# Sixteen experts' sums gathered, normed and stored in four groups of four instead of two batches

## The chip, the core and the metric

The kernel runs on one core of a Trainium2 chip. A core has TensorE (matrix products), VectorE, ScalarE and GpSimd (called POOL in the profile), each with an instruction queue of its own, worked in order, and SyncE, which here only starts transfers. Sixteen DMA engines move data between HBM and the on-chip memory. The engines meet at semaphores: an instruction or a landed transfer raises one, and another queue waits until it has a value. The metric is the device time of one execution in microseconds; smaller is better.

## The reference

Input x has 2 batches of 4096 tokens with 256 numbers each. Two layers follow each other, each as x = x + layernorm(layer(layernorm(x))). The first is a state-space layer (Mamba); the change doesn't touch it. The second is a mixture of 16 experts:

```
router_logits = silu(h @ router_w1) @ router_w2
expert_probs = softmax(router_logits.transpose(0, 2, 1), axis=-1)       # over the tokens
expert_weights, token_indices = top_k(expert_probs, 64 per batch and expert)
gate  = silu(expert_inputs @ w1);  value = expert_inputs @ w2
weighted = ((gate * value) @ w3) * expert_weights
output = zeros.at[token_indices].add(weighted)
x = x + layernorm(output)
```

A token may be chosen by several experts; their outputs are summed before the norm, so a token's norm needs its last expert. Every input and output is float32.

## The kernel before

`scan_layers` (nearly 2000 us) makes the state-space layer, the router and the part of the output that no expert touches. `experts` (L1256 to L1589) follows, and only it is changed. It handles 128 rows (64 tokens of two batches) per expert and runs these queues side by side.

VectorE ranks the logits (L1341 to L1378) and hands POOL the places of the chosen tokens in a table.

POOL starts every indirect transfer, one row per partition: `find` (L1526) fetches an expert's 128 row numbers from the table, `take` (L1529) its tokens' hidden rows and x rows, `add` (L1535) adds an expert's weighted outputs onto the rows of a sum buffer in HBM (`combine_scratch`), `gather` (L1539) reads summed rows back, `store` (L1549) writes final rows to the output. Each `take(e)` waits for its own find and is followed by `find(e + 3)`. An add waits for its expert's product (`s_y`) and for all adds before it (`d_add`), since two adds onto one row must not cross.

TensorE (L1477) makes for each expert the transposes of its tokens, `pg` (gate) and `pv` (value), and the product of the expert before. Two buffers of each let the next expert's `pg` and `pv` run while VectorE multiplies gate by value (L1421) and ScalarE makes silu (L1468) and the weighting (L1455). SyncE loads the last five experts' weights when an earlier expert's product has left its room (L1328).

Each row of the sum buffer has extra columns in which the adds leave a power of two per expert. `statistics` (L1387) reads from them whether a later expert has the same token: then this expert is a loser for the row, and its store is sent out of bounds (`dest`). So a group may be gathered when its own experts are added, and the row is stored by the last expert that holds it among those added. A later store of the same row must come after the earlier one (the wait on `d_fin`, L1554).

The sums come back in groups `GROUPS = ((0, 5), (5, 10), (10, 13), (13, 16))`. Before add 10, POOL gathers experts 0 to 9 and waits until they have landed, because add 10 changes the same rows. VectorE has `statistics(0)` behind multiply 14 and everything else behind multiply 15 (L1422 to L1434); `inverse` (L1543) is POOL's power -1/2 of the variances; `mean` (L1407) is a small VectorE step; the scaling itself is on ScalarE (`normalised`, L1457), behind the last weighting; `total` (L1413) adds x. Stores 0 to 9 stand behind adds 12 to 15 (two, two, three, three). After add 15, experts 10 to 15 are gathered, normed and stored.

## Time and profile before

| | us |
|---|---|
| median of three runs | 2185.17 |
| lowest, highest run | 2182.62, 2185.49 |
| span of the profiled execution | 2180.9 |
| busy in the span: VectorE, POOL, TensorE, ScalarE | 1878.9, 1810.3, 1681.2, 1411.6 |
| HBM read, written | 77.82 MB, 39.52 MB |

The profiled execution is one of its own; its page gives its span, from the first to the last instruction, and no further time. A run's time holds the span and what lies around it: 4.27 us between the span and the median here.

The page gives one line per group of instructions: line of the program, engine, operation, output and inputs, count, busy time, mean duration, and the idle time before. The timeline gives the instructions of one engine in order of time; what stands in brackets is the idle time before an instruction and what ended it. "issue" there means that the engine waited for nothing that the profile shows. The chain of waits goes back from the last instruction to what released it. A transfer's landing is counted from the start of the instruction that issues it.

### The profile page before, as it was taken

How to read it: one execution, taken by the hardware profiler on the slowest of the kernel's cores; microseconds unless marked ns; L12 is line 12 of the kernel's file. 1: busy time of each engine (PE TensorE's matmuls, PEld its weight loads, DVE VectorE, ACT ScalarE, POOL GpSimd, SP SyncE). 2: the span in 40 equal slices, each digit the busy share in tenths (PEclk: the TensorE clock that was granted, in tenths of full speed). 3: DMA queues.
4: the chain of work that ended last, by engine and by line, in shares of the span. 5: the costliest groups of instructions: out<-in, count | busy, mean ns of one | idle time of the engine just before them, and what ended most of it. 6: DMA issues, size and time to landing. Idle time of an engine off the chain costs nothing. (4 is left out here: it accounts for less than half of the span.)

```text
span 2180.9 us, 23218 instructions
## 1 busy us (share of the span) xinstructions
PE 1681.2 (77%) x5620; PEld 648.2 (30%) x5620; DVE 1878.9 (86%) x2070; ACT 1411.6 (65%) x2547; POOL 1810.3 (83%) x770
## 2 busy tenths in 40 slices
PE   7777879887888978788879787978888884651690
PEld 3222323232232323232323232323232231220690
DVE  2477999999999999999999999999999999996221
ACT  2565676867686768777777777776867685531121
POOL 0275999999998989898989999999999998950556
PEclk9897979889898979798979798989889895665795
DMA  2663367676667585757475656667576667427742
GB/s 92 163 181 86 88 136 158 129 159 137 146 146 154 126 175 113 167 114 166 108 159 136 146 137 144 154 136 157 126 151 148 137 139 152 110 73 234 245 106 63
DMA packets 168981, 305.16 MB, mean 140 GB/s; under 512 B 27648, under 2 KB 87810, under 8 KB 168864
## 3 DMA queue, kind: packets, MB, share of 16 engines
q1 hardware_dynamic: 137696, 240.13, 44.6%
q0 software_dynamic: 30784, 62.85, 16.1%
q10 hardware_dynamic: 384, 1.05, 0.2%
q14 instruction: 96, 0.79, 0.1%
q8 instruction: 21, 0.34, 0.1%
HBM read 77.82 MB, written 39.52 MB: 54 GB/s over the span
## 5 line engine op out<-in xcount | busy, mean ns | idle before, releaser
L1022 DVE TENSOR_TENSOR_SCAN room<-pa,carry,room 128x512 f32<-128x512 f32 x1024 | 1243.4, 1263 | 69.8 <-ACT pa L871 56.1
L1221 POOL TENSOR_TENSOR room<-room 128x2048 f32<-128x2048 f32 x256 | 1172.7, 4591 | 144.2 <-ACT carry L864 144.2
L871 ACT ACTIVATE pa<-room,neg_a 128x512 f32<-128x512 f32 x1024 | 695.1, 687 | 352.7 <-DVE room L1022 338.6
L520 PE MATMUL py<-room,blk 128*32 128x512 f32 x2048 | 338.8, 734 | 150.5 <-DVE gate L1028 95.8
L1008 DVE TENSOR_TENSOR room<-room,pb 128x2048 f32<-128x2048 f32 x192 | 434.0, 2260 | 0.8 <-DMA room<-du 0.8
L1214 POOL TENSOR_TENSOR room<-room,b_rep 128x2048 f32<-128x2048 f32 x64 | 290.3, 4536 | 6.5 <-DVE room L1022 4.6
L584 PE MATMUL pp<-xs,w_dtx 128*128 128x512 f32 x512 | 254.0, 631 | 18.0 <-DVE du L951 11.7
L593 PE MATMUL pb<-bc,sel_b 32*128 32x512 f32 x288 | 204.3, 796 | 66.2 <-DVE room L1008 66.2
L548 PE MATMUL pp<-xsp,w_conv 128*128 128x512 f32 x512 | 242.2, 606 | 8.4 <-ACT xsp L738 8.4
L540 PE MATMUL pp<-xnt,w_in 128*128 128x512 f32 x256 | 170.2, 800 | 71.7 <-ACT xs L745 59.4
L520 PEld LDWEIGHTS py<-room,blk 128*32 128x32 f32 x2048 | 44.7, 117 | 347.8 <-issue 222.5
L584 PEld LDWEIGHTS pp<-xs,w_dtx 128*128 128x128 f32 x512 | 96.4, 199 | 170.0 <-issue 142.9
L1187 POOL TENSOR_TENSOR du<-du,xs 128x512 f32<-128x512 f32 x64 | 79.7, 1263 | 74.0 <-DVE du L960 74.0
L548 PEld LDWEIGHTS pp<-xsp,w_conv 128*128 128x128 f32 x512 | 92.8, 191 | 150.1 <-issue 102.0
L564 PE MATMUL po<-xnt,w_in 128*128 128x512 f32 x240 | 125.3, 647 | 7.6 <-ACT gate L750 7.6
L607 PE MATMUL po<-w_out,gate 128*128 128x256 f32 x512 | 124.0, 391 | 4.1 <-DVE z L983 3.3
L593 PEld LDWEIGHTS pb<-bc,sel_b 32*128 32x128 f32 x288 | 51.6, 222 | 210.1 <-issue 122.8
L607 PEld LDWEIGHTS po<-w_out,gate 128*128 128x128 f32 x512 | 96.1, 193 | 51.1 <-issue 33.5
L540 PEld LDWEIGHTS pp<-xnt,w_in 128*128 128x128 f32 x256 | 55.0, 238 | 172.0 <-ACT xs L745 97.2
L745 ACT ACTIVATE xs<-pp,cb 128x512 f32<-128x512 f32 x64 | 43.6, 681 | 73.8 <-PE pp L548 69.2
L1421 DVE TENSOR_TENSOR act<-act,pv 128x512 f32<-128x512 f32 x16 | 11.0, 688 | 80.8 <-PE pv L1512 80.8
L769 ACT ACTIVATE du<-pp 128x512 f32<-128x512 f32 x64 | 38.0, 594 | 57.2 <-PE pp L584 49.5
(185 smaller groups left out, 1860.0 us busy)
## 6 DMA issues: line engine op xcount, KB each, us to landing
room<-du SPq DMA_DIRECT2D x1016, 128.0 KB, 2.4
du<-du POOLq DMA_DIRECT2D x56, 512.0 KB, 6.5
room<-in_L_ffn_w_dram SPq DMA_DIRECT2D x39, 512.0 KB, 7.4
room<-bc_scratch SPq DMA_DIRECT2D x64, 256.0 KB, 5.0
du<-late POOLq DMA_DIRECT2D x28, 512.0 KB, 6.3
combine_scratch<-zeros SPq DMA_DIRECT2D x16, 520.0 KB, 9.7
xt<-in_L_attn_x_dram SPq DMA_DIRECT2D x16, 512.0 KB, 4.4
b_rep<-bc_scratch SPq DMA_DIRECT2D x64, 128.0 KB, 5.4
```

The lines of the kernel that those rows point to most:

```text
L520: mm = pe.matmul(py[32 * j:32 * j + 32, :], blk[:], h[:, quad % 4, j, :], start=(g == 0), stop=(g == 3), tile_position=(0, 32 * j))
L540: mm = pe.matmul(pp[:], w_in[:, k, m * P:(m + 1) * P], xnt[:, k, :], start=(k == 0), stop=(k == KC - 1))
L548: mm = pe.matmul(pp[:], w_conv[:, m, tap, :], xsp[:, m % 2, tap:tap + T], start=(tap == 0), stop=(tap == TAPS - 1))
L564: mm = pe.matmul(residual_bank(i, m), w_in[:, k, DI + m * P:DI + (m + 1) * P], xnt[:, k, :], start=(k == 0), stop=(k == KC - 1))
L584: mm = pe.matmul(pp[:], w_dtx[:, k, c * P:(c + 1) * P], xs[:, k, :], start=(k == 0), stop=(k == DC - 1))
L593: pe.matmul(pb[:, bank, :], sel_b[b:b + 32, g, :], bc[b:b + 32, :], start=True, stop=True, tile_position=(b, 0)).then_inc(s_brep, 1)
L607: mm = pe.matmul(po[:, (s % 2) * DM:(s % 2 + 1) * DM], gate[:, par, k, s * P:(s + 1) * P], w_out[:, k, :], start=(k == 0), stop=(k == DC - 1))
L871: act.activation(pa[:, decay_bank(t), :], rep[:, c % 2, t % 4, 0, :], ACT.Exp, scale=neg_a[:, a_column(t):a_column(t) + 1]).then_inc(s_exp, 1)
L1008: v.tensor_tensor(bq[:, quad % 2], rep[:, c % 2, :, 1, :], pb[:, pb_bank, :].unsqueeze(1).broadcast_to((P, 4, T)), ALU.mult).then_inc(s_bd, 1)
L1022: v.tensor_tensor_scan(h[:, quad % 4, t % 4, :], pa[:, decay_bank(t), :], bq[:, quad % 2, t % 4, :], carry[:, par, t:t + 1], ALU.mult, ALU ...
L1214: pool.tensor_tensor(bq[:, 1], rep[:, c % 2, :, 1, :], b_rep[:, g // 2, :].unsqueeze(1).broadcast_to((P, 4, T)), ALU.mult).then_inc(s_bp, 1)
L1221: pool.tensor_tensor(h[:, quad % 4], h[:, quad % 4], c_rep[:, par, quad % 4, :].unsqueeze(1).broadcast_to((P, 4, T)), ALU.mult).then_inc(s ...
```

## The change

`GROUPS` becomes four groups of four. POOL gathers group g before add 4, 8 and 12 (and after add 15), waits for the landing ahead of that add, makes the group's power two experts later (or at the end), and stores its rows two behind each of two adds. The statistics of a group stand on VectorE behind the multiply two experts after the group, its mean, its norm (now on VectorE, four `tensor_scalar`) and its sums behind the multiply after that, but none later than behind multiply 15. ScalarE's `normalised` goes. The row numbers are copied to float per group. Of the finds ahead of the first take, two remain instead of three; a take is followed by `find(e + 2)`.

```
-    GROUPS = ((0, 5), (5, 10), (10, 13), (13, 16))
-    HALF = 10
+    GROUPS = ((0, 4), (4, 8), (8, 12), (12, 16))
+    STATS_AFTER, TOTAL_AFTER = 2, 3
+    STORES_AFTER = {6: (0, 1), 7: (2, 3), 10: (4, 5), 11: (6, 7), 14: (8, 9), 15: (10, 11)}
...
                 def statistics(g):
                     first, stop = GROUPS[g]
-                    if g == 0:
-                        v.tensor_copy(rowf[:], rowid[:]).then_inc(s_lose, 1)
                     v.wait_ge(d_cb[g], 16 * (stop - first))
+                    v.tensor_copy(rowf[:, first:stop], rowid[:, first:stop])
...
+                    v.wait_ge(s_lose, g + 1)
+                    v.scalar_tensor_tensor(out=dest[:, first:stop], in0=loser[:, first:stop], scalar=float(2 * B * S),
+                                           in1=rowf[:, first:stop], op0=ALU.mult, op1=ALU.add).then_inc(s_dest, 1)
                     v.wait_ge(s_f, 2 * g + 2)
                     v.tensor_scalar(fvar[:, first:stop], fmv[:, first:stop, 1], EPS, None, ALU.add).then_inc(s_fv, 1)
...
+                def total(g):
                     first, stop = GROUPS[g]
                     v.wait_ge(s_fp, g + 1)
                     v.scalar_tensor_tensor(out=fnm[:, first:stop], in0=fmv[:, first:stop, 0], scalar=-1.0,
                                            in1=frs[:, first:stop], op0=ALU.mult, op1=ALU.mult).then_inc(s_fn, 1)
-                def total(g):
-                    for e in range(*GROUPS[g]):
+                    v.wait_ge(s_fn, g + 1)
+                    for e in range(first, stop):
+                        v.tensor_scalar(comb[:, e, 0:DM], comb[:, e, 0:DM], frs[:, e:e + 1], fnm[:, e:e + 1], ALU.mult,
+                                        ALU.add).then_inc(s_fa, 1)
+                    for e in range(first, stop):
                         v.wait_ge(s_fa, e + 1)
                         v.tensor_tensor(comb[:, e, 0:DM], comb[:, e, 0:DM], taken[:, e, DM:], ALU.add).then_inc(s_fo, 1)
...
                     v.tensor_tensor(act1[:, e % 2, :], act1[:, e % 2, :], pv[:, e % 2, :], ALU.mult).then_inc(s_m, 1)
-                    if e == 14:
-                        statistics(0)
-                statistics(1)
...
-                total(3)
+                    for g, (_, stop) in enumerate(GROUPS[:-1]):
+                        if e == min(stop + STATS_AFTER, E - 1):
+                            statistics(g)
+                        if e == min(stop + TOTAL_AFTER, E - 1):
+                            total(g)
+                statistics(len(GROUPS) - 1)
+                total(len(GROUPS) - 1)
...
-                for g in range(len(GROUPS)):
-                    normalised(g)
...
-                    if e + 3 < E:
-                        find(e + 3)
+                    if e + 2 < E:
+                        find(e + 2)
...
-                for e in range(3):
+                for e in range(2):
                     find(e)
...
                 for e in range(E):
+                    before = [g for g, (_, stop) in enumerate(GROUPS) if stop == e]
+                    for g in before:
+                        pool.wait_ge(d_add, 16 * e)
+                        for done in range(*GROUPS[g]):
+                            gather(done)
                     if e + LOOK < E:
                         take(e + LOOK)
+                    for g, (_, stop) in enumerate(GROUPS[:-1]):
+                        if e == stop + STATS_AFTER:
+                            inverse(g)
                     pool.wait_ge(s_y, e + 1)
                     if e > 0:
                         pool.wait_ge(d_add, 16 * e)
-                    if e == HALF:
-                        for first in range(HALF):
-                            gather(first)
-                        for g in range(2):
-                            pool.wait_ge(d_cb[g], 16 * 5)
+                    for g in before:
+                        pool.wait_ge(d_cb[g], 16 * (GROUPS[g][1] - GROUPS[g][0]))
                     add(e)
...
+                    for done in STORES_AFTER.get(e, ()):
+                        store(done)
                 pool.wait_ge(d_add, 16 * E)
-                for e in range(HALF, E):
+                for e in range(*GROUPS[-1]):
                     gather(e)
-                inverse(2)
-                inverse(3)
-                for e in range(HALF, E):
+                inverse(len(GROUPS) - 1)
+                for e in range(*GROUPS[-1]):
                     store(e)
```

## Rows read from the trace of the kernel before

**Rows 1.** Stage table: stretch, us, busy of PE, PEld, DVE, ACT, POOL, granted clock, DMA, GB/s.

```profile
2048.00:2079.00 31.00, 31.00 (x243) 29.97 (x243) 3.44 (x5) 7.92 (x18) 14.44 (x14) 1.00 0.98 312
...
2152.00:2172.00 20.00, 0.00 (x0) 0.00 (x0) 6.08 (x26) 3.16 (x6) 12.95 (x14) 0.50 0.24 76
```

**Rows 2.** Chain that ended last: start us, us, what; adds, then gathers, then add 10.

```profile
2093.20 3.84 DMA combine_scratch<-comb,rowid
...
2097.82 3.86 DMA combine_scratch<-comb,rowid
...
2107.10 0.98 POOL comb L1541
...
2110.90 0.95 POOL comb L1541
...
2118.40 2.79 DMA comb<-combine_scratch,rowid
...
2121.95 3.93 DMA combine_scratch<-comb,rowid
```

**Rows 3.** Timeline of POOL, first finds and first take: start us, us, line, operation, tiles.

```profile
2027.07 1.09 POOL L1527 DMA_INDIRECT rowid<-token_table,entry  x1 [44.54 <-DVE entry L1362]
...
2029.75 0.94 POOL L1527 DMA_INDIRECT rowid<-token_table,entry  x1 [0.30 <-issue]
2030.99 0.95 POOL L1531 DMA_INDIRECT taken<-hidden_scratch,rowid  x1 [0.30 <-issue]
```

**Rows 4.** DMA issues: the first find, then the third; last number: us to landing.

```profile
rowid<-token_table,entry POOLq DMA_INDIRECT x1, 3.1
...
rowid<-token_table,entry POOLq DMA_INDIRECT x1, 2.3
```

**Rows 5.** Timeline of POOL: add 4, take, find; adds 12 and 13 with two stores between.

```profile
2078.97 1.62 POOL L1536 DMA_INDIRECT combine_scratch<-comb,rowid  x1 [3.61 <-DMA combine_scratch<-comb,rowid]
2080.90 0.98 POOL L1531 DMA_INDIRECT taken<-hidden_scratch,rowid  x1 [0.30 <-issue]
2082.19 0.95 POOL L1527 DMA_INDIRECT rowid<-token_table,entry  x1 [0.30 <-issue]
...
2131.23 1.73 POOL L1536 DMA_INDIRECT combine_scratch<-comb,rowid  x1 [0.62 <-DVE comb L1416]
...
2136.00 1.57 POOL L1536 DMA_INDIRECT combine_scratch<-comb,rowid  x1 [0.39 <-issue]
```

**Rows 6.** Timeline of POOL, the end: last power, first and last of six stores.

```profile
2163.00 0.85 POOL L1546 TENSOR_TENSOR frs<-fvar,mhalf 128x3 f32<-128x3 f32 x1 [2.65 <-DVE fvar L1402]
2165.05 1.05 POOL L1555 DMA_INDIRECT out_dram<-comb,dest  x1 [1.20 <-DVE comb L1416]
...
2171.51 0.97 POOL L1555 DMA_INDIRECT out_dram<-comb,dest  x1 [0.30 <-issue]
```

**Rows 7.** Timeline of VectorE: multiply 7, ten sums, last group's statistics, sums of experts 10 to 12.

```profile
2079.36 0.69 DVE L1421 TENSOR_TENSOR act<-act,pv 128x512 f32<-128x512 f32 x1 [4.83 <-PE pv L1512]
...
2130.73 4.46 DVE L1416 TENSOR_TENSOR comb<-comb,taken 128x256 f32<-128x256 f32 x10
...
2161.29 1.08 DVE L1394 BATCH_NORM_STATS2 fst<-comb 128x6 f32<-128x256 f32 x3 [2.08 <-DMA comb<-combine_scratch,rowid]
...
2163.72 1.41 DVE L1416 TENSOR_TENSOR comb<-comb,taken 128x256 f32<-128x256 f32 x3 [0.67 <-ACT comb L1460]
```

**Rows 8.** Timeline of TensorE: product 7, products 14 and 15.

```profile
2084.61 1.89 PE L1497 MATMUL pY<-room,act 128*128 128x256 f32 x8
...
2123.02 3.62 PE L1497 MATMUL pY<-room,act 128*128 128x256 f32 x16
```

**Rows 9.** Groups by line and form: busy us, mean ns of one, idle before.

```profile
L1197 POOL TENSOR_TENSOR rs<-var,mhalf 128x4 f32<-128x4 f32 x32 | 33.0, 1031 | 23.5 <-ACT var L824 23.5
...
L1130 DVE TENSOR_SCALAR w_conv<-ident,cw 128x128 f32<-128x128 f32 x16 | 3.2, 279 | 0.0
...
L1124 DVE TENSOR_SCALAR w_in<-w_in,rms 128x1024 f32<-128x1024 f32 x2 | 1.4, 749 | 2.7 <-DMA w_in<-in_L_attn_W_in_dram 2.7
```

More of the change, by code:

```diff
@@ L1311, in experts @@
         s_bit, s_lose, s_dest = sem("bits_step"), sem("losers_step"), sem("dest_ready")
-        s_f, s_fv, s_fp, s_fn, s_fa, s_fo = (sem("final_stats_step"), sem("final_variance"), sem("final_pow"), sem("final_mean"),
-                                             sem("final_normalised"), sem("final_sum"))
+        s_fv = sem("final_variance")
+        s_f, s_fp, s_fn, s_fa, s_fo = (sem("final_stats_step"), sem("final_pow"), sem("final_mean"), sem("final_normalised"),
+                                       sem("final_sum"))
         def weights(e):
@@ L1400, in statistics @@
                     ins.then_inc(s_f, 1)
+                    v.wait_ge(s_lose, g + 1)
+                    v.scalar_tensor_tensor(out=dest[:, first:stop], in0=loser[:, first:stop], scalar=float(2 * B * S),
+                                           in1=rowf[:, first:stop], op0=ALU.mult, op1=ALU.add).then_inc(s_dest, 1)
                     v.wait_ge(s_f, 2 * g + 2)
                     v.tensor_scalar(fvar[:, first:stop], fmv[:, first:stop, 1], EPS, None, ALU.add).then_inc(s_fv, 1)
-                    v.wait_ge(s_lose, g + 2)
-                    v.scalar_tensor_tensor(out=dest[:, first:stop], in0=loser[:, first:stop], scalar=float(2 * B * S),
-                                           in1=rowf[:, first:stop], op0=ALU.mult, op1=ALU.add).then_inc(s_dest, 1)
-                def mean(g):
+                def total(g):
                     first, stop = GROUPS[g]
@@ L1421, in _ @@
                     v.tensor_tensor(act1[:, e % 2, :], act1[:, e % 2, :], pv[:, e % 2, :], ALU.mult).then_inc(s_m, 1)
-                    if e == 14:
-                        statistics(0)
-                statistics(1)
-                mean(0)
-                mean(1)
-                total(0)
-                total(1)
-                statistics(2)
-                statistics(3)
-                mean(2)
-                total(2)
-                mean(3)
-                total(3)
+                    for g, (_, stop) in enumerate(GROUPS[:-1]):
[5 more added lines that the diff above has]
+                total(len(GROUPS) - 1)
             @block.scalar
@@ L1455, in weighted @@
                     act.activation(comb[:, e, 0:DM], pY[:, e % 2, 0:DM], ACT.Identity, scale=weight[:, e:e + 1]).then_inc(s_y, 1)
-                def normalised(g):
-                    act.wait_ge(s_fn, g + 1)
-                    for e in range(*GROUPS[g]):
-                        act.activation(comb[:, e, 0:DM], comb[:, e, 0:DM], ACT.Identity, scale=frs[:, e:e + 1],
-                                       bias=fnm[:, e:e + 1]).then_inc(s_fa, 1)
                 copied(0)
@@ L1549, in store @@
                 def store(e):
-                    pool.wait_ge(s_dest, group(e) + 1)
+                    g = group(e)
+                    if e == GROUPS[g][0]:
+                        pool.wait_ge(s_dest, g + 1)
+                        if e > 0:
+                            pool.wait_ge(d_fin, 16 * e)
                     pool.wait_ge(s_fo, e + 1)
-                    if e == HALF:
-                        pool.wait_ge(d_fin, 16 * HALF)
                     pool.indirect_dma_start(outf, at(dest, e), comb[:, e, 0:DM], None, bounds_check=B * S - 1,
@@ L1570, in _ @@
                         pool.wait_ge(d_add, 16 * e)
-                    if e == HALF:
-                        for first in range(HALF):
-                            gather(first)
-                        for g in range(2):
-                            pool.wait_ge(d_cb[g], 16 * 5)
-                    add(e)
-                    if e == 11:
-                        inverse(0)
-                        inverse(1)
-                    for first in {12: (0, 1), 13: (2, 3), 14: (4, 5, 6), 15: (7, 8, 9)}.get(e, ()):
-                        store(first)
+                    for g in before:
+                        pool.wait_ge(d_cb[g], 16 * (GROUPS[g][1] - GROUPS[g][0]))
+                    add(e)
+                    for done in STORES_AFTER.get(e, ()):
+                        store(done)
                 pool.wait_ge(d_add, 16 * E)
-                for e in range(HALF, E):
+                for e in range(*GROUPS[-1]):
                     gather(e)
-                inverse(2)
-                inverse(3)
-                for e in range(HALF, E):
+                inverse(len(GROUPS) - 1)
+                for e in range(*GROUPS[-1]):
                     store(e)
```

## The prediction

> **What bounds the kernel now.** Read the stage table first [rows 1]: it gives each engine's busy time, TensorE's granted clock and the DMA share by stretch. The change touches only the last 155 us of a span of 2180.9, so the shares of the whole span tell nothing here. From 2048 to 2079 the DMA engines are full with the experts' last weights (share 0.98). TensorE's last product ends at 2126.64 [rows 8], and from 2152 it has no work at all while POOL is busy 12.95 us of 20: the end is set by POOL's queue. Then the chain of waits [rows 2]: the adds stand one behind another, since each waits until the one before has landed (3.84 us from issue, then 0.78 to the next start: 4.62 per add, against the products' 5.52 per expert, which is 0.69 + 4.83 in VectorE's row [rows 7]). At 2107 ten gathers go out, 1.27 apart; the last lands 2.79 after its issue, and the next add starts at 2121.95. That break cost 14.85. The adds are late by then (product 7 ends at 2086.5 [rows 8], add 7 starts at 2093.20), so the whole stretch from add 4 to the last store is one serial POOL chain: 2078.97 to 2171.51, 92.54 us [rows 5, 6]. I cost the change by laying out that same chain anew.
>
> **The first take, one issue sooner.** One find of three goes, so the first take could start at 2029.75 rather than 2030.99 [rows 3], 1.24 sooner. But it needs the first find, which lands 3.1 after its start at 2027.07 [rows 4], at 2030.17; with the 0.76 to 0.78 that POOL took from a landing to the next start [rows 2] that is 2030.9. I take a gain of 0.1; bounds 0 and 1.24. The later finds keep their number.
>
> **The chain, anew.** Adds 0 to 3 and the weights' stream have the same waits as before; I leave them where they are. Add 3 then frees not add 4 but the first gather, so at 2078.97. The prices: gathers 1.27 apart, from the first gather of a group to the add after it 3.80 + 3.55 = 7.35, where 3.80 is three spacings and 3.55 is 2118.40 to 2121.95 [rows 2]; add to next instruction 1.93, take 1.29, find 1.25 (0.95 busy and 0.30 idle) [rows 5]; store 1.29 (6.46 for five) [rows 6]; add to add 4.62 [rows 2], with two stores between 4.77 (2131.23 to 2136.00) [rows 5]; the power of four columns 1.03 [rows 9].
> Gathers 0 to 3, take 10, find 12, add 4: POOL's own work binds, 5.05 + 1.29 + 1.25 = 7.59, beside the landing's 7.35.
> Add 4 to 5: 4.62.
> Add 5 to 6: take, find and the power lie between: 1.93 + 1.29 + 0.95 + 1.03 + 0.30 = 5.50. Issue binds, no longer the landing.
> Add 6 to 7: stores 0 and 1, take 13, find 15: 1.93 + 2.58 + 1.29 + 1.25 = 7.05.
> Add 7 to gather 4, two stores: 4.77. Gathers to add 8: 7.35 (take 14 is under the landing).
> Adds 8 to 9 to 10: 9.24 (take 15 and the second power are covered by landings).
> Add 10 to 11 to gather 8, two stores each: 9.54. Gathers to add 12: 7.35.
> Adds 12 to 13 to 14: 9.24, power covered. Add 14 to 15 to gather 12, two stores each: 9.54.
> Gather 12 to the last landing: 3.80 + 2.79 = 6.59.
> Landing to the first of the last stores: for three experts VectorE needed 1.71 until the power began (2161.29 to 2163.00) [rows 6, 7]; for four I add 0.36 for one more statistics, 0.10 for its aggregate, 0.08 for the row numbers now copied there: 2.25. Power 1.03, mean 0.20. Then the norm on VectorE, four scalings of 256 columns: no row shows this form; of the same operation 128 columns took 0.28 and 1024 took 0.75 [rows 9], so 0.35 alone, less back to back; I take 0.30, 1.20 for four (bounds 0.8 and 1.4). First sum 0.44 (4.46 for ten [rows 7]), and 0.89 to the store (the sum of expert 10 ends at 2164.16, its store starts at 2165.05 [rows 6, 7]). Sum 6.01. Three more stores: 3.87.
> Together 98.26 against 92.54: 5.7 longer. What makes it up: three breaks of 7.35 to 7.59 for one of 14.85 (+7.4) and the stores and power between adds 5 and 7 (+3.3), against two gathers and two stores fewer at the end (-5.1), two spans of three stores between adds that now hold two, and a longer last group of statistics.
>
> **What VectorE's waits do.** VectorE has the product of gate and value in the same order, so whatever it waits for holds the products. The statistics of group 0 stand behind multiply 6 and wait for gather 3, landed at 2085.56 (2078.97 + 3.80 + 2.79); with 2.25 on top multiply 7, which ran at 2079.36 [rows 7], starts at 2087.8 and product 7, which ran at 2084.61 [rows 8], at 2088.6. The sums of group 0 stand behind it and wait for the power, done at 2096.4; with mean, four norms and four sums (3.16) multiply 8 comes at 2099.5 and product 8 some 10 us late. ScalarE loses 16 scalings, off the path; it isn't free for longer than the products let it. None of this is on the chain: expert 8 is ready at 2102.5 and add 8 goes at 2115.9, 13 us to spare; expert 15 waits for gather 11 (2141.2), statistics, multiply and product, some 2146.5, and add 15 goes at 2156.0, 9.5 to spare. If that cover were gone, every us of it would be a us at the end.
>
> **A rule weighed.** A POOL issue beside VectorE's work took 1.73 where others took 1.57 and 1.62 (the add at 2131.23 beside the ten sums) [rows 5, 7], 0.1 to 0.2 more. The norms of group 0 fall beside add 6, the one place where issue binds; I leave this in the bounds.
> The Trainium skill, "SBUF — State Buffer", section "SBUF: two separate sides", states that VectorE in a two-port mode holds the port that GpSimd needs to write its DMA descriptors, and GpSimd stands still until it ends; "Who interferes with whom" there counts scaling by a scalar among such operations. By that rule add 6 would wait for four norms, and the time would be that of the second rival; the 1.73 agrees in sign, though the sums read two tensors and are not scalings, and no run here shows a norm beside an issue.
>
> **The sum against the median.** The profiled execution's span is 2180.9; the median of the runs is 2185.17, so 4.27 lies around it, if that execution was a usual one. The span becomes 2186.5, the time 2185.17 + 5.7 - 0.1 = 2190.8.
>
> **The rivals.**
> The last gathers land sooner in small groups: not slower. Its place is the wait after the fourth gather, which binds at groups 2, 3 and 4. For: the finds land in 2.3 to 3.1, less than 2.79 at best [rows 4]. Against: they move 4 bytes a row. At 2.3 the gain is 3 x 0.49 = 1.5 and the time 2189.3; below a landing of 2.34 the change is no longer measurable. The first take's whole 1.24 would give 2189.6, the edge of the same.
> The norms hold POOL: the four scalings of 0.30 in front of add 6 cost up to 1.2: 2192.0. For: the 1.73. Against: nothing else overlaps so.
> TensorE becomes the bound. Its granted clock was 1.00 (2.4 GHz) with the products running and 0.50 (1.2 GHz) with TensorE idle [rows 1]. If VectorE's waits drop it at product 8 and it doesn't rise again, seven experts take twice 5.52: 2100.2 + 77.3 = 2177.5 where add 15 wants 2156.0, 22 more: 2213. It decides once 9.5 us are lost. Against: the stalls are of 4 to 10 us with products between.
> That the new order removes more than I see, and it is faster: I find no wait of the old chain that goes without one in its place, but the end has two gathers and two stores less, 5.1, if the early breaks were covered by slack. For that the adds would have to wait for products, and before they don't.
>
> **How the numbers follow.** Forecast 0.58 (2188.5 to 2192.5, most of it above). Sooner landings 0.12; norms holding POOL 0.12; TensorE bound 0.08; something faster or level that I don't see 0.10. About 0.2% (4.4 us, up to 2189.5) is what a measurement can tell from no change. Slower: 0.45 of the forecast + 0.12 + 0.08 = 0.65. Within: 0.13 + 0.12 + 0.04 = 0.29. Faster: 0.06. The range takes in the bounds (below, the first take -1.2, landings -1.5, the five two-store steps at 4.62 instead of 4.77 -0.8, of which not all come together; above, the held issue 1.2 and a part of TensorE's case): 2187.0 to 2195.5.
>
> **What would show it.** First take at 2030.9, not 2029.8. Three breaks of about 7.4 in the adds, each from a landed add to the next. 5.5 and 7.0 between adds 5, 6 and 7. Multiplies 7 and 8 at 2087.8 and 2099.5, TensorE idle before products 7 and 8, its last product near 2146. Last gather to last store start 2.79 + 6.01 + 3.87. If add 15 waits for its product, or the adds after a group start below 7 us from its first gather, I am wrong.

## The result, and the profile after

The changed kernel takes 2192.32 us (median of six, 2188.48 to 2196.30) against 2185.57 (six, 2182.62 to 2188.45): a ratio of 1.003, 95% interval 1.0016 to 1.0044, or 6.7 us slower. The forecast was 2190.8, range 2187.0 to 2195.5, slower.

The whole time is a coarse measure here. Where a profile's own run time is known (2193.58 for the changed kernel's, with a span of 2191.8), the time is the start of the first find, the stretch from it to the last store's start, and 11.2 us (11.15 to 11.24 in the thirteen profiles that have both). The first find starts anywhere between 2026.2 and 2036.4, though nothing ahead of it differs between these kernels. So I compare the stretch from the first find to the start of the last store, and call it the stage: 144.44 in the kernel before (2027.07 to 2171.51 [rows 3, 6]), 151.24 in the changed one, and 151.11 in a second profile of it. The 6.8 us agree with the medians.

The stage has a loose part of its own. Up to the start of what add 3 frees (gather 0 in the changed kernel, add 4 in the one before) it took 48.9 to 53.0 us in twelve profiles, the two paced kernels below aside; in the profiles of the kernel before and of second_break, whose programs are the same up to there, it took 51.90 and 52.95. So a difference of a us or two between two stages has to be looked up in the steps. From the first gather on, the two profiles of the changed kernel took 101.09 and 101.34. One run of second_break, 2531.39 us at a granted clock of 0.625, was slow and is left out of its median.

Stage table of the changed kernel, the columns of [rows 1]: stretch, length, busy of PE, PEld, DVE, ACT, POOL with counts, granted clock, DMA share, GB/s. Its stage begins 4.04 us later in its span; the stretches take that in.

```profile
2052.00:2083.00 31.00, 31.00 (x238) 29.84 (x238) 3.44 (x5) 7.53 (x17) 13.88 (x13) 1.00 0.94 304
2083.00:2126.00 43.00, 35.45 (x237) 32.97 (x236) 10.26 (x38) 7.66 (x18) 30.93 (x29) 0.88 0.40 89
2126.00:2156.00 30.00, 19.42 (x111) 16.78 (x110) 9.77 (x33) 3.69 (x9) 17.30 (x14) 0.88 0.32 57
2156.00:2176.00 20.00, 0.00 (x0) 0.00 (x0) 3.05 (x16) 0.00 (x0) 12.47 (x11) 0.50 0.29 65
```

TensorE now works up to 2151.8 instead of 2126.64 [rows 8] and stands still 7.6 us of the 43 from 2083 to 2126; its mean granted clock there is 0.88, where it was 1.00 in the stretch ahead. In the last 20 us it again has nothing, while POOL is at work.

Timeline of POOL in the changed kernel, answering [rows 3, 5, 6]: start us, us, line, operation, tiles, idle before and what ended it. L1517 is `find`, L1521 `take`, L1526 `add`, L1531 `gather`, L1536 the power, L1547 `store`.

```profile
2031.11 1.09 POOL L1517 DMA_INDIRECT rowid<-token_table,entry  x1 [44.54 <-DVE entry L1364]
...
2034.88 0.95 POOL L1521 DMA_INDIRECT taken<-hidden_scratch,rowid  x1 [1.40 <-DMA rowid<-token_table,entry]
...
2081.26 0.99 POOL L1531 DMA_INDIRECT comb<-combine_scratch,rowid  x1 [3.15 <-DMA combine_scratch<-comb,rowid]
...
2088.84 1.63 POOL L1526 DMA_INDIRECT combine_scratch<-comb,rowid  x1 [0.30 <-issue]
...
2099.00 1.65 POOL L1526 DMA_INDIRECT combine_scratch<-comb,rowid  x1 [0.19 <-issue]
2101.78 1.03 POOL L1547 DMA_INDIRECT out_dram<-comb,dest  x1 [1.14 <-DVE comb L1420]
...
2107.02 1.63 POOL L1526 DMA_INDIRECT combine_scratch<-comb,rowid  x1 [0.30 <-ACT comb L1453]
...
2115.41 0.95 POOL L1531 DMA_INDIRECT comb<-combine_scratch,rowid  x1 [0.30 <-issue]
...
2119.70 1.62 POOL L1526 DMA_INDIRECT combine_scratch<-comb,rowid  x1 [2.09 <-DMA comb<-combine_scratch,rowid]
...
2128.90 2.52 POOL L1526 DMA_INDIRECT combine_scratch<-comb,rowid  x1 [1.90 <-DMA combine_scratch<-comb,rowid]
...
2174.49 1.05 POOL L1536 TENSOR_TENSOR frs<-fvar,mhalf 128x4 f32<-128x4 f32 x1 [4.05 <-DVE fvar L1406]
2178.42 1.04 POOL L1547 DMA_INDIRECT out_dram<-comb,dest  x1 [2.89 <-DVE comb L1420]
...
2182.35 0.98 POOL L1547 DMA_INDIRECT out_dram<-comb,dest  x1 [0.30 <-issue]
```

The first break is seen from the gather at 2081.26 to the add at 2088.84; the second ends with the last of its gathers at 2115.41 and the add at 2119.70. Between adds 6 and 7 (2099.00 and 2107.02) lie 8.02 us. The add at 2128.90 (add 10) is busy for 2.52 where others take 1.6.

Timeline of VectorE, answering [rows 7]: L1393 begins the statistics, L1425 is the multiply of gate and value, L1411 the mean, L1416 the norm, L1420 the sums.

```profile
2087.87 0.17 DVE L1393 CAST rowf<-rowid 128x4 f32<-128x4 uint32 x1 [10.56 <-DMA comb<-combine_scratch,rowid]
...
2089.87 0.69 DVE L1425 TENSOR_TENSOR act<-act,pv 128x512 f32<-128x512 f32 x1
2098.84 0.16 DVE L1411 SCALAR_TENSOR_TENSOR fnm<-fmv,frs 128x4 f32<-128x4 f32 x1 [8.29 <-POOL frs L1536]
2099.04 1.50 DVE L1416 TENSOR_SCALAR comb<-comb,frs,fnm 128x256 f32<-128x256 f32 x4
2100.46 1.42 DVE L1420 TENSOR_TENSOR comb<-comb,taken 128x256 f32<-128x256 f32 x4
...
2128.53 1.42 DVE L1420 TENSOR_TENSOR comb<-comb,taken 128x256 f32<-128x256 f32 x4
```

VectorE waits 10.56 us for the gathers ahead of multiply 7 and 8.29 for the power ahead of multiply 8. TensorE's products 7, 8 and 15:

```profile
2090.61 3.64 PE L1487 MATMUL pY<-room,act 128*128 128x256 f32 x8 [3.06 <-DVE act L1425]
...
2102.53 3.78 PE L1487 MATMUL pY<-more,act 128*128 128x256 f32 x8 [4.49 <-DVE act L1425]
...
2148.28 3.51 PE L1487 MATMUL pY<-room,act 128*128 128x256 f32 x8 [3.20 <-DVE act L1425]
```

Products 7 and 8 wait 3.06 and 4.49 us for their multiply and take 3.64 and 3.78 where 1.89 was usual [rows 8].

### The profile page after: what moved, and what is told of

It is laid out like the page before. It is cut to its first block and busy times, and to the rows that moved or that the text cites. A ratio compares the mean times of both kernels' runs of the same rounds, so it can differ in the third digit from the quotient of the medians.

```text
span 2191.8 us, 23208 instructions
## 1 busy us (share of the span) xinstructions
PE 1690.6 (77%) x5620; PEld 653.8 (30%) x5620; DVE 1883.0 (86%) x2089; ACT 1403.9 (64%) x2531; POOL 1812.2 (83%) x770
## 3 DMA queue, kind: packets, MB, share of 16 engines
q10 hardware_dynamic: 384, 1.05, 0.2%
## 5 line engine op out<-in xcount | busy, mean ns | idle before, releaser
L593 PEld LDWEIGHTS pb<-bc,sel_b 32*128 32x128 f32 x288 | 51.6, 222 | 209.6 <-issue 123.5
L564 PEld LDWEIGHTS po<-xnt,w_in 128*128 128x128 f32 x240 | 45.5, 206 | 87.8 <-issue 68.5
```

Source lines behind the costliest of these rows:

```text
L564: mm = pe.matmul(residual_bank(i, m), w_in[:, k, DI + m * P:DI + (m + 1) * P], xnt[:, k, :], start=(k == 0), stop=(k == KC - 1))
L593: pe.matmul(pb[:, bank, :], sel_b[b:b + 32, g, :], bc[b:b + 32, :], start=True, stop=True, tile_position=(b, 0)).then_inc(s_brep, 1)
```

## The experiments

In each, the stage is read from one profile and the ratio is to the kernel before, run beside it. Those runs beside had medians of 2185.73 (changed_again, vector_unheld, stores_later, norm_scalar), 2186.27 (take_alone, second_break, paced_weights, one_break) and 2187.04 (the other four), so the medians of the table are compared by the ratios alone. The third column is the start of the first gather, counted from the first find; the stage less that is the stretch from the first gather on.

| kernel | stage, us | first gather, us | median, us | ratio, 95% interval |
|---|---|---|---|---|
| before | 144.44 | 80.03 | 2185.57 | |
| changed | 151.24 | 50.15 | 2192.32 | 1.0030 (1.0016 to 1.0044) |
| changed_again | 151.11 | 49.77 | 2191.97 | 1.0035 (1.0022 to 1.0048) |
| vector_unheld | 160.27 | 49.70 | 2198.02 | 1.0058 (1.0045 to 1.0071) |
| vector_unheld_2 | 150.57 | 48.92 | 2194.81 | 1.0035 (1.0023 to 1.0048) |
| stores_later | 147.56 | 51.50 | 2188.01 | 1.0011 (1.0002 to 1.0019) |
| norm_scalar | 149.34 | 50.52 | 2190.10 | 1.0025 (1.0015 to 1.0036) |
| norm_sum_in_turn | 148.12 | 49.73 | 2189.61 | 1.0009 (1.0000 to 1.0018) |
| take_alone | 144.38 | 79.61 | 2183.42 | 0.9986 (0.9976 to 0.9996) |
| second_break | 146.85 | 57.18 | 2186.85 | 1.0001 (0.9990 to 1.0012) |
| paced_weights | 142.50 | 77.67 | 2185.29 | 0.9993 (0.9981 to 1.0004) |
| one_break | 144.92 | 79.39 | 2186.09 | 0.9994 (0.9981 to 1.0007) |
| one_break_scalar | 141.35 | 79.93 | 2180.47 | 0.9965 (0.9952 to 0.9978) |
| one_break_scalar_paced | 140.41 | 77.42 | 2179.37 | 0.9958 (0.9945 to 0.9970) |

The theory: the end is set by POOL's serial chain, and the changed kernel is slower by its two more breaks and by what lies in POOL's queue between adds. The rivals: the products, held by VectorE's waits, cost the time; VectorE's new work beside POOL's issues costs it; something ahead of the stage does.

**changed_again.** The changed kernel, with no edit.

> The changed kernel once more, beside the three below on one chip. The first profile had the experts' stage beginning 4.04 us later than in the profile of before, with nothing changed ahead of it. If that is chance from one execution to the next, the first find starts elsewhere again and the stage from first find to last store stays at 151.2 us (144.4 in the kernel before): 0.25 to 0.35% slower than before. If the change delays what lies ahead of it, the first find starts at about 2031 again.

The first find starts at 2027.39 this time, the stage is 151.11. What lies ahead of the stage is not the change's doing.

**vector_unheld.** VectorE's part in the changed kernel:

```
-                    for g, (_, stop) in enumerate(GROUPS[:-1]):
-                        if e == min(stop + STATS_AFTER, E - 1):
-                            statistics(g)
-                        if e == min(stop + TOTAL_AFTER, E - 1):
-                            total(g)
+                    if e == 8:
+                        statistics(0)
+                    if e == 10:
+                        total(0)
+                    if e == 14:
+                        statistics(1)
+                total(1)
+                statistics(2)
+                total(2)
```

> Changed kernel with VectorE's statistics and sums moved behind later multiplies (statistics of group 0 behind multiply 8, its sums behind 10, statistics of group 1 behind 14, the rest behind 15), POOL's order untouched. Theory of POOL's chain: TensorE loses its stalls of 3 to 4.5 us and ends 15 to 20 us sooner, the last store stays within 1 us: slower than before by 5.5 to 7.5 us. Rival, the held products set the end: the time falls by 4 us or more, to at most +2.5.

Neither theory said 160.27. The edit put in a wait that I had not seen. TensorE's transposes of expert 14, and POOL's second power, in the timelines of TensorE and POOL:

```profile
2125.95 0.69 PE L1482 MATMUL pt<-ident,taken 128*128 128x128 f32 x2 [6.39 <-DMA taken<-hidden_scratch,rowid]
```

```profile
2139.37 1.04 POOL L1540 TENSOR_TENSOR frs<-fvar,mhalf 128x4 f32<-128x4 f32 x1 [8.13 <-DVE fvar L1406]
```

With its stalls gone TensorE reaches expert 14 before POOL has taken its tokens and waits 6.39 us; multiply 14 comes late, the statistics of group 1 stand behind it, and POOL waits 8.13 us for their variance. It is a loop between POOL's late takes and POOL's own power. It says nothing of the theories, so the edit was mended.

**vector_unheld_2.** The same, with group 1 one and two multiplies sooner:

```
-                    if e == 14:
-                        statistics(1)
-                total(1)
+                    if e == 12:
+                        statistics(1)
+                    if e == 13:
+                        total(1)
```

> As vector_unheld, but with the statistics of group 1 behind multiply 12 and its sums behind 13, so that POOL's second power doesn't wait for a multiply that itself waits for a late take. Theory of POOL's chain: TensorE's last product starts at about 106 us after the first find instead of 117, the last store stays at 151 (150 to 152). Rival, the held products cost the time: the last store comes sooner by more than 3.

TensorE's last two products, and POOL's add 10 and last store:

```profile
2136.76 3.62 PE L1492 MATMUL pY<-room,act 128*128 128x256 f32 x16
```

```profile
2130.07 2.45 POOL L1531 DMA_INDIRECT combine_scratch<-comb,rowid  x1 [1.98 <-DMA combine_scratch<-comb,rowid]
...
2183.37 0.98 POOL L1552 DMA_INDIRECT out_dram<-comb,dest  x1 [0.30 <-issue]
```

TensorE ends at 2140.38, 107.6 after the first find (2032.80), where the changed kernel needs 120.7 (2151.79 less 2031.11); multiplies 7 and 8 run at their usual times. The stage is 150.57, within 0.7 of the changed kernel (from the first gather on it is 101.65, 0.3 to 0.6 longer), and the ratio is 1.0035 as in changed_again. The products held by VectorE cost the kernel nothing that can be seen. Add 10 still takes 2.45.

**stores_later.**

```
-    STORES_AFTER = {6: (0, 1), 7: (2, 3), 10: (4, 5), 11: (6, 7), 14: (8, 9), 15: (10, 11)}
+    STORES_AFTER = {8: (0,), 9: (1,), 10: (2, 3), 11: (4, 5), 12: (6, 7), 14: (8, 9), 15: (10, 11)}
```

> Changed kernel with stores 0 to 7 placed where an add or a group of gathers lands anyway: store 0 after add 8, 1 after 9, 2 and 3 after 10, 4 and 5 after 11, 6 and 7 between gather 11 and add 12. Theory of POOL's chain: add 6 to add 7 falls from 8.0 to 4.6 us, the other steps stay: 3.4 sooner than the changed kernel, some +3.3 against before. Rival, VectorE's norms hold POOL's issue: add 6 stays long and little is gained, under 1.5.

POOL from add 6 to add 7:

```profile
2101.83 1.66 POOL L1526 DMA_INDIRECT combine_scratch<-comb,rowid  x1 [0.19 <-issue]
2103.80 1.13 POOL L1521 DMA_INDIRECT taken<-hidden_scratch,rowid  x1 [0.30 <-issue]
2105.23 0.96 POOL L1517 DMA_INDIRECT rowid<-token_table,entry  x1 [0.30 <-issue]
2106.55 1.62 POOL L1526 DMA_INDIRECT combine_scratch<-comb,rowid  x1 [0.36 <-issue]
```

4.72 instead of 8.02, 3.30 less where 3.4 was counted; the stage loses 3.6 (147.56), the median 4.0 to 4.3. One line that moves stores gives back half of the change's loss. From the first gather on the gain is 5.0 to 5.3: the second break took 7.34 for 8.11, and add 10, which began 0.40 behind the start of a row of norms and ran beside that, 1.61 for 2.52. No power or store lies in front of add 7 now; the power in front of add 6 still does (5.44).

**second_break.** In the kernel before:

```
+                    if e == 5:
+                        pool.wait_ge(d_add, 16 * 5)
+                        for first in range(5):
+                            gather(first)
...
-                        for first in range(HALF):
+                        for first in range(5, HALF):
```

> Kernel before with its one break of ten gathers ahead of add 10 made into two of five, ahead of adds 5 and 10; VectorE, ScalarE and the products untouched (one store moved by one add so that stores of a row keep their order). Theory of POOL's chain: 8.84 (issue of five gathers, take, find) and 8.63 in place of 14.85, 2.6 us slower. Rival, the changed kernel is slower by VectorE's work between the products and not by the breaks: no change.

POOL from the first gather of the new break to add 5:

```profile
2093.55 0.99 POOL L1541 DMA_INDIRECT comb<-combine_scratch,rowid  x1 [2.61 <-DMA combine_scratch<-comb,rowid]
...
2098.60 0.95 POOL L1541 DMA_INDIRECT comb<-combine_scratch,rowid  x1 [0.30 <-issue]
2099.85 0.94 POOL L1531 DMA_INDIRECT taken<-hidden_scratch,rowid  x1 [0.30 <-issue]
2101.10 0.94 POOL L1527 DMA_INDIRECT rowid<-token_table,entry  x1 [0.30 <-issue]
2102.35 1.61 POOL L1536 DMA_INDIRECT combine_scratch<-comb,rowid  x1 [0.30 <-issue]
```

The new break takes 8.80 (2093.55 to 2102.35), as counted (8.84), and the other 8.03 where 8.63 was counted (last gather to add 2.98). Together they take 1.98 more than the one of 14.85. The stage grows by 2.4, but 1.05 of that lies ahead of add 4, where nothing was changed; from add 4 to the last store it is 93.90 for 92.54. The whole times can't show so little: 1.0001, within 0.0012. A break of its own, with VectorE, ScalarE and products as before, so costs about 2 here, of which 1.4 reached the last store, and the changed kernel has two more breaks than the kernel before.

**take_alone.**

```
-                    if e + 3 < E:
-                        find(e + 3)
+                    if e + 2 < E:
+                        find(e + 2)
...
-                for e in range(3):
+                for e in range(2):
                     find(e)
```

> Kernel before with the first take one issue sooner, nothing else. In five profiles of the changed kernel and its variants the first take starts 3.03 to 3.77 us after the first find (3.92 in the kernel before), and the fourth add frees its successor 49.7 to 51.5 after it (51.9). Theory: the first find's landing binds, so the gain is 0.2 to 0.9 us, no more than a measurement can tell, and add 4 varies by as much from run to run. Rival, the full issue counts: 1.2 to 1.8 us sooner, in every profile.

```profile
2026.21 1.10 POOL L1527 DMA_INDIRECT rowid<-token_table,entry  x1 [44.55 <-DVE entry L1362]
...
2029.66 0.94 POOL L1531 DMA_INDIRECT taken<-hidden_scratch,rowid  x1 [1.08 <-DMA rowid<-token_table,entry]
```

The first take starts 3.45 after the first find instead of 3.92: it waits 1.08 for the find, as 1.40 in the changed kernel. Over all kernels with two finds ahead it starts after 3.03 to 3.77, so the gain is 0.15 to 0.9, set by the find's landing. Add 4 starts at 51.63 after the first find (51.90 before), and the stage ends at 144.38 against 144.44. The whole times say 0.14% sooner, and their interval, 0.9 to 5.2 us sooner, excludes no change and takes in the rival's 1.2 to 1.8. But the take itself is only 0.47 sooner and the one profiled stage 0.06, so where the gain comes from stays open. Whether a sooner take shortens the adds beside the weights stays open too: where add 3 frees its successor lies at 48.9 to 51.6 in all ten profiles with two finds, and at 51.9 and 53.0 in the two with three (the paced kernels aside).

**norm_scalar.** In the changed kernel `normalised` is back on ScalarE, for groups 0 and 1 in iterations 9 and 13, for the others at the end; VectorE's four `tensor_scalar` of each group go.

```
+                    if e in (9, 13):
+                        normalised(e // 4 - 2)
                     if e > 0:
                         weighted(e - 1)
                 weighted(E - 1)
+                normalised(2)
+                normalised(3)
```

> Changed kernel with the sixteen scalings back on ScalarE (groups 0 and 1 ahead of the weighting of experts 8 and 12, the others behind the last one); all else unchanged. Theory of POOL's chain: within 1 us of the changed kernel, since ScalarE's four take about 2.0 against 1.4 to 1.5 on VectorE. Rival, VectorE's two-port scalings hold POOL's issue: adds 6, 10 and 14 take 1.6 instead of 1.65, 2.52 and 1.91, steps 10 to 11 and 13 to 14 lose 0.5 to 0.9 each, 1.5 to 2.5 sooner in all. If add 10 stays at 2.5, it is the sums of two tensors that hold it.

Add 10:

```profile
2126.78 1.81 POOL L1533 DMA_INDIRECT combine_scratch<-comb,rowid  x1 [1.94 <-DVE comb L1417]
```

The stage is 1.8 to 1.9 shorter (149.34), from the first gather on 2.3 to 2.5, the rival's size. Add 10 falls from 2.43 and 2.52 to 1.81, step 10 to 11 from 5.39 and 5.48 to 4.88; store 0 waits for its sum less long (step 6 to 7 is 7.31 for 8.02); and at the end the last gather's start is followed by the first store after 8.28 instead of 8.93, which fits ScalarE's scalings and VectorE's sums overlapping. So the place of the norm costs about 2 us. Which of VectorE's two rows holds POOL isn't told apart by this.

**one_break.** Norm and sum on VectorE as in the changed kernel, one break of ten as before, and POOL's stores packed:

```
+    GROUPS = ((0, 5), (5, 10), (10, 13), (13, 16))
+    HALF = 10
+    STORES_AFTER = {11: (0, 1), 12: (2, 3), 13: (4, 5), 14: (6, 7), 15: (8, 9)}
...
+                inverse(2)
+                for e in range(HALF, E):
+                    if e == HALF + 2:
+                        inverse(3)
                     store(e)
```

> Norm and sum on VectorE and the sooner take as in the changed kernel, but one break of ten gathers as in the kernel before; statistics of groups 0 and 1 behind multiply 14, two stores behind each of adds 11 to 15 (so no add is held by three), and the power of the last three experts after store 11, so that store 10 need not wait for it. Theory of POOL's chain: the steps from add 14 to 15 and to gather 10 fall from 5.8 to 4.7 each, the first of the last stores starts 2 us sooner: 3 to 4 us faster than before. Rival, VectorE's work beside POOL's issues gives it back: within 1.5 of before.

VectorE's sums of group 0, norms and sums of group 1 (L1416 norm, L1420 sum), and POOL's add 11 and stores 0 and 1:

```profile
2129.69 1.76 DVE L1420 TENSOR_TENSOR comb<-comb,taken 128x256 f32<-128x256 f32 x5
...
2131.56 1.95 DVE L1416 TENSOR_SCALAR comb<-comb,frs,fnm 128x256 f32<-128x256 f32 x5
2133.43 1.75 DVE L1420 TENSOR_TENSOR comb<-comb,taken 128x256 f32<-128x256 f32 x5
```

```profile
2129.53 3.43 POOL L1528 DMA_INDIRECT combine_scratch<-comb,rowid  x1 [0.36 <-issue]
2133.26 2.84 POOL L1549 DMA_INDIRECT out_dram<-comb,dest  x1 [0.30 <-issue]
2136.40 1.00 POOL L1549 DMA_INDIRECT out_dram<-comb,dest  x1 [0.30 <-issue]
```

The rival: nothing gained (from the first gather on 65.53, where the kernel before took 64.41). Add 11 is busy 3.43 and store 0 2.84, together 3.7 over their usual time; the steps from add 14 to 15 and to the gathers behind it fell to 4.62 and 4.50, as counted. Laid beside VectorE's rows: the sums end at 2131.45 and add 11 ends 1.5 later, about a whole add's issue (1.57), while the norms from 2131.56 on run beside it. The next sums end at 2135.18 and store 0 ends 0.9 later, about a whole store's issue. In the changed kernel add 10 (2128.90 to 2131.42) ends 1.47 after the sums that end at 2129.95. By these ends, POOL's issue begins when the row of sums is over; beside norms it isn't lengthened (add 6, at 2099.00 beside the norms at 2099.04: 1.65; add 10 of stores_later, begun inside such a row: 1.61).

**norm_sum_in_turn.** In the changed kernel each sum comes right behind its norm:

```
                     for e in range(first, stop):
                         v.tensor_scalar(comb[:, e, 0:DM], ...).then_inc(s_fa, 1)
-                    for e in range(first, stop):
                         v.wait_ge(s_fa, e + 1)
                         v.tensor_tensor(comb[:, e, 0:DM], ...).then_inc(s_fo, 1)
```

> Changed kernel with VectorE's norm and sum of one expert after the other instead of four norms and then four sums. In the changed kernel add 10 ended 1.47 us after the last of four back-to-back sums in two profiles, and one_break's first store 0.9 after five of them, while norms alone ran beside an add without lengthening it. If the row of sums holds POOL's issue, adds 10 and 14 take under 2.0 instead of 2.4 to 2.5; if the scalings hold it, they stay at 2.4 or more. The first last store comes 0.5 to 1 sooner, since its sum need not wait for four norms. Stage 149.5 to 150.5 instead of 151.2.

VectorE's last two pairs of group 1 and POOL's add 10:

```profile
2128.52 0.41 DVE L1416 TENSOR_SCALAR comb<-comb,frs,fnm 128x256 f32<-128x256 f32 x1
2128.97 0.42 DVE L1419 TENSOR_TENSOR comb<-comb,taken 128x256 f32<-128x256 f32 x1
2129.31 0.69 DVE L1416 TENSOR_SCALAR comb<-comb,frs,fnm 128x256 f32<-128x256 f32 x1
2130.03 0.43 DVE L1419 TENSOR_TENSOR comb<-comb,taken 128x256 f32<-128x256 f32 x1
```

```profile
2128.70 1.70 POOL L1525 DMA_INDIRECT combine_scratch<-comb,rowid  x1 [1.98 <-DVE comb L1419]
```

Add 10 takes 1.70 and add 14 1.73, with norms and sums both still on VectorE and both beside the add. So it is sums in an unbroken row that hold POOL, not the scalings. Here it is a norm that is lengthened beside the add, 0.69 for the usual 0.41. The gain is larger than forecast, 3.0 (148.12): the first sum of a group is ready after one norm, so store 0 doesn't wait any more (step 6 to 7 is 7.19) and the last stores begin 8.04 after the last gather's start instead of 8.93.

**one_break_scalar.** one_break with the scalings on ScalarE, groups 0 and 1 ahead of the weighting of expert 14, and the means of groups 0 and 1 ahead of both groups' sums, as in the kernel before.

> one_break with the scalings on ScalarE (groups 0 and 1 ahead of the weighting of expert 14, the others at the end). In one_break add 11 took 3.43 and the first store 2.84, 3.7 more than their usual 1.57 and 1.00. Theory, VectorE's row of sums and norms held them: both fall to under 2.0 and 1.2, and the stage ends at 141 to 142 after the first find (144.9 in one_break, 144.4 in before): about 3 us or 0.14% faster than before. Rival, POOL was held by the order of its own queue: no change against one_break.

VectorE's sums of groups 0 and 1, POOL's add 11, store 0 and the last store:

```profile
2131.02 4.46 DVE L1417 TENSOR_TENSOR comb<-comb,taken 128x256 f32<-128x256 f32 x10
```

```profile
2131.61 1.65 POOL L1540 DMA_INDIRECT combine_scratch<-comb,rowid  x1 [0.71 <-DVE comb L1417]
2133.57 1.04 POOL L1561 DMA_INDIRECT out_dram<-comb,dest  x1 [0.30 <-DVE comb L1417]
...
2173.06 0.98 POOL L1561 DMA_INDIRECT out_dram<-comb,dest  x1 [0.30 <-issue]
```

The sums stand 0.45 apart again. Add 11 takes 1.65, store 0 1.04, and the stage is 141.35: 3.1 less than before (3.0 from the first gather on), at 0.9965 (0.9952 to 0.9978). It is faster than both kernels. The whole times give more than the stage does, 4.8 us at the least; what is beyond 3.1 isn't explained: nothing ahead of the stage was edited, and the stage is known from one execution. Against the kernel before, the stage gains by two stores behind each of five adds, and by a power that stands between the last stores instead of ahead of them.

**paced_weights.** In the kernel before:

```
-                    if e >= RING:
-                        sp.wait_ge(s_o, e - RING + 1)
-                    for w, dst in zip((w1, w2, w3), weights(e)):
+                    for k, (w, dst) in enumerate(zip((w1, w2, w3), weights(e))):
+                        if e >= RING:
+                            sp.wait_ge(s_o, 1 + 2 * (e - RING) + k // 2)
```

> Kernel before with the last five experts' weights spread out: the three transfers of expert 11 + k wait for 1 + 2k, 1 + 2k and 2 + 2k products instead of 1 + k, so they end some 20 us later and still 10 us or more before they are read. Theory: adds 0 to 3 landed after 5.8 to 7.3 us because the weights filled the DMA engines; with half of that load they land in 4 to 5, the adds keep up with the products (5.52 apart) to add 9, the break begins at 76 instead of 80 after the first find, and the end is 3 to 4.5 us sooner. Rival: POOL's queue is late for its own number of issues, and nothing moves.

Add 4 and the first gather (first find at 2036.02):

```profile
2080.15 1.62 POOL L1536 DMA_INDIRECT combine_scratch<-comb,rowid  x1 [1.00 <-ACT comb L1455]
...
2113.69 0.98 POOL L1541 DMA_INDIRECT comb<-combine_scratch,rowid  x1 [4.11 <-DMA combine_scratch<-comb,rowid]
```

Add 4 comes 7.8 sooner after the first find (44.13), but the spread weights now meet adds 4 to 9, which take 4.7 to 7.0 a step, and the break begins only 2.4 sooner (77.67), the stage ends 1.9 sooner. Add 6 starts 0.29 after the weighting of its own product, so by then the adds had caught up with the products. Less than forecast: the load wasn't lessened, it was moved along the same chain.

**one_break_scalar_paced.** Both edits together.

> one_break_scalar with the last experts' weights spread out as in paced_weights, where add 4 came 7.8 us sooner after the first find, the break 2.4 sooner and the last store 1.9 sooner. If both gains are on one chain they add: last store at 138.5 to 140 after the first find, about 5 us or 0.23% faster than before. If the later adds lose to the weights what the first ones gain, it stays at 141 or more.

The stage is 140.41, 0.9 less than without the pacing, between the two forecasts. Up to the first gather the gains add: it starts 2.5 sooner than without the pacing (77.42 for 79.93), as 2.4 in paced_weights. The break then loses 1.6: its last gather landed after 4.8 instead of 3.2 and is followed by add 10 after 5.5 instead of 3.9. No weights move there (the DMA view of 2107.3 to 2124.2 has no packet of the weights' queue); what falls into that landing is told under the breaks below. The ratio, 0.9958 (0.9945 to 0.9970), can't be told from that of one_break_scalar.

## Why the prediction was right, step by step

Steps of the stage in us, as the prediction put them and as the changed kernel's timeline has them:

| step | predicted | measured |
|---|---|---|
| first find to first gather | 51.8 | 50.15 |
| gather 0 to add 4 | 7.59 | 7.58 |
| add 4 to 5, 5 to 6 | 4.62, 5.50 | 4.71, 5.45 |
| add 6 to 7 | 7.05 | 8.02 |
| add 7 to gather 4 | 4.77 | 4.57 |
| gather 4 to add 8 | 7.35 | 8.11 |
| add 8 to 10 | 9.24 | 9.20 |
| add 10 to gather 8 | 9.54 | 9.98 |
| gather 8 to add 12 | 7.35 | 7.42 |
| add 12 to 14 | 9.24 | 9.84 |
| add 14 to gather 12 | 9.54 | 9.51 |
| gather 12 to last landing | 6.59 | 6.66 |
| landing to first of the last stores | 6.01 | 6.11 |
| three more stores | 3.87 | 3.93 |
| stage | 150.1 | 151.24 |

**What bounds.** Right: POOL's chain. vector_unheld_2 freed the products and gained nothing; stores_later moved stores, and the step that they had held became 3.30 shorter where 3.4 was counted.

**The breaks.** Right in size: the first took 7.58, the third 7.42. The second was 0.76 longer because its last gather landed after 3.5 (VectorE's statistics begin at 2118.92) and not 2.79; in stores_later and the two vector_unheld this break took 7.3 to 7.4, in the other variants of the changed kernel 8.1 to 8.6. The DMA views show what goes with it. The fourteen profiles have 43 groups of gathers. In 33 of them no packet of the two queues that the page calls instruction (q8 and q14) lies between the last gather's start and its landing, and that landing took 2.7 or 2.8 us; in the ten others there is at least one, and it took 2.8 to 4.8. The four long second breaks (3.5 to 4.0) each have a packet of q8, one_break_scalar_paced's 4.8 has both kinds. That these packets are the cause is not shown: no run moved them. The rival of sooner landings didn't come: none was below 2.7. second_break shows the price of a break alone.

**The first take.** Right: set by the find's landing, 2034.88 less 4.04 is 2030.84 where 2030.9 was said.

**Adds 0 to 3.** I left them where they were. They ended 1.65 sooner than that, and 0.3 to 3.0 sooner in all kernels with two finds. Only 0.15 of it is the first take's in this profile. That it hid the next terms is luck: from the first gather on, the chain took 101.09 and 101.34 where 98.26 was forecast, so it grew by 8.5 to 8.8 and not by 5.7, while the stage came out 1.1 above the forecast. Add 6 to 7 (1.0), the late landing (0.8) and the adds held by sums (1.0, in the steps from adds 10 and 12) make up most of that difference.

**Add 6 to 7.** Mis-sized by 1.0. I let store 0 be free by the time POOL reached it. Four norms (1.50) ahead of the first sum and 0.88 from the sum to the store made POOL wait 1.14. The prediction had that 0.88 at the end of the stage and not here; by its own prices (power done at 2096.4, then 0.20, 1.20, 0.44 and 0.89, against add 6 at 2096.68 and 1.93) store 0 would have been 0.5 late already.

**VectorE's work beside POOL.** The rival was named, with the wrong culprit: it blamed the scalings, at add 6, up to 1.2. Add 6 was untouched; adds 10 and 14 lost up to 0.9 to the sums. Before, the sums stood 0.45 apart, spaced by ScalarE [rows 7]; moved behind norms on the same engine they stand 0.35 apart, and that row POOL's issue doesn't pass. In the Trainium skill, "SBUF — State Buffer", "Who interferes with whom", a sum of two on-chip tensors contends with GpSimd's reads, and by inference leaves its descriptor writing alone, while scalings can hold it. In these runs the row of sums held the issue (2.43 to 3.43 for an add instead of 1.57) and no scaling was seen to (1.65 and 1.61 beside four of them). That rival's time, 2192.0, lies near the measured one by chance: its mechanism wasn't seen.

**VectorE's waits.** Right: multiply 7 at 2085.83 and 8 at 2097.76 on the scale of the profile before (4.04 taken off), 2.0 and 1.7 sooner than said because the gathers were, and a last product that leaves 8.8 us to add 15 (9.5 said). The rival of TensorE as the bound came as far as its first step: the granted clock fell to 0.50 at products 7 and 8, but it rose again behind each, and add 15 didn't wait for its product.

**Span and time.** Wrong: I took 4.27 us to lie around the span. It is 1.78 (2193.58 less 2191.8), and 1.7 to 1.8 in all thirteen profiles that have both, so the profiled execution of before took an estimated 2182.7, 2.5 below the median. The difference of the two kernels doesn't depend on it.

## What to carry to other kernels

When one queue works a serial chain of transfers that wait for each other, price every insertion by what the landings can hide: two stores fit under one add here, a third or a take beside them went into the time whole. Splitting one round trip into three costs the fixed part of a trip each time (about 2 us here), and moving work to an earlier place gains only where the queue that carries it has idle landings; the gaps of other engines are no room. Before moving work onto an engine, look at what its new neighbours in that queue do to the order and spacing of what it already did. And hold a forecast against its steps, not only against its sum: here errors of opposite sign left the sum right.

## What the runs showed of the hardware

Indirect transfers issued by GpSimd were held for as long as VectorE ran sums of two on-chip tensors in an unbroken row: add 11 3.43 and store 0 2.84 in one_break, add 10 2.43 to 2.52 in the changed kernel, each ending 1.5 (a store 0.9) after the row. With norms between the sums add 10 took 1.70, and beside a row of four norms an add took 1.65 (add 6) and 1.61 (add 10 of stores_later). That the issue waits for its read of the row numbers on the chip is argued, not shown.

TensorE's first products after a stall of 3.06 and 4.49 us took 3.64 and 3.78 instead of 1.89. The granted clock was 0.50 (1.2 GHz) from 2090.60 to 2092.40 and from 2102.50 to 2106.20, while these products ran, and 1.00 (2.4 GHz) from 2094.20 to 2096.00 and from 2108.70 to 2110.70. The second stall slowed the gate product behind it too (2.68 for 1.95), so the stalls cost 1.75 and about 2.6 us more than their length.

A group's last gather landed in 2.7 or 2.8 us where no packet of the instruction queues fell into its flight (33 cases), and in 2.8 to 4.8 where one did (ten).

What lies ahead of the first find (state-space layer, router, ranking), the same in all kernels, took from 2026.2 to 2036.4 us in the profiles.
